# Gathered rows of a three-layer graph network: written-out layers, a ring of eight groups, and first groups that gather x itself

## The reference

```python
msg = relu((x[src] * edge_weight[:, None]) @ W_msg + b_msg)          # layer 0
agg = segment_sum(msg, dst, N)
x1  = layernorm(x + relu(agg @ W_out + b_out))
# layers 1 and 2, h = x1 and then the result of layer 1
msg = einsum('nd,rde->rne', h, W)[edge_type, src]
h   = relu(segment_sum(msg, dst, N) + h @ SW + b)
out = layernorm(x1 + h)                                               # after layer 2
```

## Time and profile before

| | |
|---|---|
| median of 3 runs | 7518.52 us (7510.16 to 7519.22) |
| span of the profiled execution, first to last instruction | 6622.7 us |
| own time of the profiled execution | not given apart from its span |
| runs' median less the profiled span | 895.8 us |
| POOL busy | 4948.3 us (75%) |
| PE busy | 3199.1 us (48%), mean granted clock 0.583 |
| DVE busy | 1746.3 us (26%) |
| ACT busy | 686.1 us (10%) |
| instructions executed | 52,372 |

### The profile page before, as it was taken

The page is one execution under the profiler, slowest core; times in us unless marked ns, Lnnn a source line. Parts: engine busy times, 40 slices in busy tenths (PEclk is TensorE's granted clock), DMA queues, the critical chain, the costliest instruction groups (busy, mean ns, idle before and its releaser), DMA issues. The chain is left out here.

```text
span 6622.7 us, 52372 instructions
## 1 busy us (share of the span) xinstructions
PE 3199.1 (48%) x12124; PEld 2491.7 (38%) x12124; DVE 1746.3 (26%) x4136; ACT 686.1 (10%) x2063; POOL 4948.3 (75%) x5004
## 2 busy tenths in 40 slices
PE   4455555555555444444445544443444444443443
PEld 4344444444444333333333333333333333333333
DVE  3344444444444311111111111111111111111112
ACT  1112222222222100000000000000000000000000
POOL 4777777777777677777777777767777777777776
PEclk7566666656666656666665666665555555555555
DMA  4122222222222222222222222221222222222222
GB/s 130 52 80 83 83 83 83 83 83 83 83 83 87 76 54 76 76 75 75 75 72 76 76 75 76 76 77 50 56 57 58 58 58 57 57 57 56 58 57 55
DMA packets 255517, 474.23 MB, mean 72 GB/s; under 512 B 90635, under 2 KB 143412, under 8 KB 255454
## 3 DMA queue, kind: packets, MB, share of 16 engines
q0 software_dynamic: 159744, 327.48, 19.1%
q1 hardware_dynamic: 92620, 144.65, 6.0%
q10 hardware_dynamic: 3090, 1.38, 0.1%
HBM read 351.16 MB, written 121.98 MB: 71 GB/s over the span
## 5 line engine op out<-in xcount | busy, mean ns | idle before, releaser
L576 POOL DMA_INDIRECT rows<-rel_table,index x3328 | 3306.4, 994 | 1070.0 <-issue 1009.7
L622 PE MATMUL bank<-onehot,rows 128*128 128x128 f32 x9984 | 2337.4, 408 | 3369.7 <-DMA rows<-rel_table,index 2340.9
L622 PEld LDWEIGHTS bank<-onehot,rows 128*128 128x128 f32 x9984 | 2024.6, 301 | 3668.2 <-DMA rows<-rel_table,index 1590.4
L576 POOL DMA_INDIRECT rows<-msg_table,index x1664 | 1629.8, 979 | 587.6 <-issue 583.3
L608 DVE TENSOR_TENSOR agg<-agg,bank 128x128 f32 x624 | 179.5, 288 | 3569.0 <-PE bank L622 3540.5
L596 DVE SCALAR_TENSOR_TENSOR rows<-rows,weight,bm 128x128 f32<-128x128 f32 x1664 | 474.6, 347 | 1146.8 <-DMA rows<-msg_table,index 1146.8
L584 DVE TENSOR_TENSOR onehot<-columns,place 128x1024 f32<-128x1024 f32 x624 | 765.8, 1227 | 19.6 <-issue 9.7
L819 PE MATMUL bank<-wr,feat 128*128 128x512 f32 x784 | 641.8, 969 | 3.5 <-ACT feat L767 2.4
L568 ACT ACTIVATE rows<-rows 128x512 f32<-128x512 f32 x416 | 261.8, 629 | 1657.9 <-DVE rows L596 1657.9
L819 PEld LDWEIGHTS bank<-wr,feat 128*128 128x128 f32 x784 | 236.9, 332 | 198.8 <-issue 194.6
L559 ACT ACTIVATE index<-rel_index 128x8 int32 (+1 forms) x416 | 85.4, 207 | 1546.4 <-DMA rows<-rel_table,index 1542.3
(11 more groups left out here) (65 smaller groups left out, 628.6 us busy)
## 6 DMA issues: line engine op xcount, KB each, us to landing
rel_table<-tab SPq DMA_DIRECT2D x196, 512.0 KB, 2.7
rows<-rel_table,index POOLq DMA_INDIRECT x3328, 2.5
rows<-msg_table,index POOLq DMA_INDIRECT x1664, 2.5
x_dram<-normed SPq DMA_DIRECT2D x98, 64.0 KB, 2.9
xin<-x_dram SPq DMA_DIRECT2D x98, 64.0 KB, 2.0
xin<-in_x_dram SPq DMA_DIRECT2D x97, 64.0 KB, 2.4
out_dram<-normed SPq DMA_DIRECT2D x97, 64.0 KB, 2.0
tab<-in_x_dram SPq DMA_DIRECT2D x24, 256.0 KB, 2.8
```

Of the source, the lines that this page charges most:

```text
L576: nc.gpsimd.indirect_dma_start(rows[:, st.u, t, :], None, table, bass.IndirectOffsetOnAxis(ap=index[:, st.u, t:t + 1], axis=0)).then_inc(s ...
L622: ins = nc.tensor.matmul(ps_edge[k][:, 0:P], rows[:, st.u, t, :], onehot[:, k, t, :], start=t == 0, stop=t == TPG - 1)
```

## The change

1. `RING` = 8: `rows` holds 8 groups. The second chunk of raw edges and the sheets' transposes now live in memory that is free at that time (`spare`, `raws[0][0]`).
2. All three layers are written out (`fused_loop` has no hardware loop), and so is `message_table`. POOL's gathers take their row numbers straight from `msg_index` or `rel_index` (`static_gather`). The executed path no longer uses `index`. The program has 26,781 instructions where it had 8447.
3. The first 8 groups (`EARLY`) gather rows of x, as soon as their numbers are laid out, ahead of the window check (`early_gathers`). On arrival PE transposes them and multiplies them by W_msg (`pe_convert`, `act_convert`), and DVE scales the product out of PSUM.
4. `columns` and `bm` are copied to PSUM (`ps_columns`, `ps_bm`, bank 5). `onehot` and the scaling of all groups but the first 8 read them there. `ps_a` is left with one bank, so a block's product waits for the `y` of the block before.
5. The layout copies src first, and transposes each part as soon as it is there; the window check comes after `message_table`. ACT zeroes `agg` in 25 pieces within `message_table`.

```diff
+RING = 2 * UNROLL
...
-        rows = sb("rows", [P, UNROLL, TPG, D])
+        rows = sb("rows", [P, RING, TPG, D])
...
-        ps_a = [bank[4], bank[5]]
+        ps_a = bank[4]
         ps_t = [bank[6], bank[7]]
+        ps_sheet = [bank[4], bank[5]]
+        ps_columns = bank[5][:, 0:P]
+        ps_bm = bank[5][:, P:P + D]
...
+                nc.vector.tensor_copy(f_src, e_src).then_inc(sems.flt, 1)
...
-                nc.vector.tensor_copy(f_src, e_src)
...
-        IDX_LEAD = 2
+        IDX_LEAD = 3
+        EARLY = RING
...
+        def static_gather(layer, g):
...
+            u = g % RING
+            table, table_index = ((rel_tables[layer - 1], rel_index) if layer else
+                                  (x if g < EARLY else msg_table, msg_index))
+            n = layer * GROUPS + g
+            need(nc.gpsimd, edge_main.prod, n - RING + 1)
+            pass_waits(nc.gpsimd, s_pool_turn)
+            for t in range(TPG):
+                nc.gpsimd.indirect_dma_start(
+                    rows[:, u, t, :], None, table,
+                    bass.IndirectOffsetOnAxis(ap=table_index[:, g, t:t + 1], axis=0)
+                ).then_inc(s_early[u] if n < EARLY else edge_main.rows[u][t // HALF], 16)
+
+        def early_gathers():
...
+            nc.gpsimd.wait_ge(lay.te, 2)
+            for g in range(EARLY):
+                if g == RING // 2:
+                    nc.gpsimd.wait_ge(lay.te, BATCHES * IN_ORDER)
+                    nc.gpsimd.wait_ge(lay.flag, 1)
+                static_gather(0, g)
+
+        def pe_convert(g):
...
+            for h in range(2):
+                i = 2 * g + h
+                if h == 0:
+                    nc.tensor.wait_ge(s_early[g], 16 * TPG)
+                need(nc.tensor, s_feat, i - 1)
+                for j in range(HALF):
+                    ins = nc.tensor.transpose(ps_t[h][:, j * P:(j + 1) * P],
+                                              rows[:, g, h * HALF + j, :], ident[:, :])
+                ins.then_inc(s_turned, 1)
+            for h in range(2):
+                i = 2 * g + h
+                nc.tensor.wait_ge(s_feat, i + 1)
+                need(nc.tensor, edge_main.scaled, i - 1)
+                for j in range(HALF):
+                    ins = nc.tensor.matmul(ps_tab[h][:, j * D:(j + 1) * D],
+                                           sheet_feat[:, h, j * P:(j + 1) * P], wm[:, :],
+                                           start=True, stop=True)
+                ins.then_inc(s_product, 1)
...
-                in0=columns[:, :].unsqueeze(1).to_broadcast([P, TPG, P]),
+                in0=ps_columns.unsqueeze(1).to_broadcast([P, TPG, P]),
...
-                            out=rows[:, st.u, t, :], in0=rows[:, st.u, t, :],
-                            scalar=w[:, 0, t:t + 1], in1=bm[:, :], op0=ALU.mult, op1=ALU.add)
+                            out=rows[:, st.u, t, :],
+                            in0=product if convert else rows[:, st.u, t, :],
+                            scalar=w[:, 0, t:t + 1],
+                            in1=bm[:, :] if convert else ps_bm, op0=ALU.mult, op1=ALU.add)
...
+                    piece = agg[:, st.b * ZERO:min((st.b + 1) * ZERO, NP + P)]
+                    eng.activation(piece, ones[:, 0:1].to_broadcast([P, piece.shape[1]]), ACT.Copy,
+                                   scale=0.0).then_inc(s_zero, 1)
...
-                need(nc.tensor, sems.xuse, st.n - 1)
+                need(nc.tensor, sems.xuse, st.n)
...
+            steps = GROUPS // PAIR if eng is nc.gpsimd else BLOCKS + LAG + LAST_STAGE[layer]
+            for s in range(steps):
+                at = At(s - s % UNROLL, s % UNROLL)
+                fused_edges(eng, layer, s)
+                if eng is nc.scalar and at.block(LAG, BLOCKS) is not None:
+
+                    eng.wait_ge(edge_main.added, min(s * PAIR + 1, GROUPS) + layer * GROUPS)
                 node_step(eng, layer, at, LAG)
...
-            eng.memset(agg[:, :], 0.0).then_inc(s_zero, 1)
+            early_gathers()
```

More of the change, by code:

```diff
@@ L36, with __init__ @@
 class Block:
-    def __init__(self, b, first, u):
+    def __init__(self, b, first, u, ring=UNROLL, early=0):
         self.b = b
         self.n = b + first
-        self.u = u % UNROLL
+        self.u = u % ring
+        self.early = early
 class At:
@@ L551, in gathered, with act_index @@
         def gathered(st):
-            return (st.n - st.u + UNROLL) * (16 * HALF // UNROLL)
-        def act_index(layer, sems, st, lead):
+            return (st.n - st.u + RING * (1 - st.early)) * (16 * HALF // RING)
+        def act_index(layer, sems, step, lead, first):
             table_index = msg_index if layer == 0 else rel_index
[L557 to L560, removed]
+            for q in range(PAIR):
+                k = step.u * PAIR + q
+                last = Block(step.b * PAIR + (q - RING), first, k, RING)
+                if isinstance(last.n, int) and last.n < 0:
+                    continue
+                for h in range(2):
+                    nc.scalar.wait_ge(sems.rows[k][h], gathered(last))
+            nc.scalar.activation(
+                index[:, step.u, :],
+                table_index[:, at_index(step.b * PAIR + lead, PAIR), :].rearrange(
+                    "p g t -> p (g t)"), ACT.Copy).then_inc(sems.index, 1)
         def act_relu(layer, sems, st):
@@ L581, in dve_group, with act_convert @@
+        def act_convert(g):
+            for h in range(2):
+                i = 2 * g + h
+                nc.scalar.wait_ge(s_turned, i + 1)
+                need(nc.scalar, s_product, i - 1)
+                nc.scalar.activation(sheet_feat[:, h, :], ps_t[h][:, :], ACT.Copy
+                                     ).then_inc(s_feat, 1)
         def dve_group(layer, sems, st, lead):
@@ L645, in edge_step @@
                 elif st is not None:
-                    if eng is nc.gpsimd:
-                        pool_gather(layer, sems, st, lead)
+                    if eng is nc.scalar:
+                        act_relu(layer, sems, st)
+                    elif eng is nc.gpsimd:
+                        pool_gather(layer, sems, st, at.block(0, steps, first // PAIR))
                     elif eng is nc.tensor:
@@ L732, in emit @@
                     ins.then_inc(s.prod, 1)
[L734 to L736 removed]
+            for n in range(SHEETS + (eng is nc.tensor)):
+                emit(At(n - n % UNROLL, n % UNROLL))
         PRODUCTS = (3, 0)
```

197 lines of the change are left out of this document (121 added, 76 removed).

## The result

| | before | changed |
|---|---|---|
| median of 3 runs | 7518.52 us (7510.16 to 7519.22) | 7324.3 us (7323.71 to 7329.33) |
| ratio | | 0.9747 [0.9729, 0.9764] |
| profiled execution: own time, span | not given, 6622.7 us | 7329.33 us, 7327.3 us |

The account below looks back on a forecast made before the run. The prediction took a chain of 4992 gathers on POOL to bound the kernel. Its terms, -70.5 - 197 + 3 = -264.5, taken from 7518.5, gave 7254.0 us, with a range of 7185 to 7400.

Parts of the forecast that it names:

- three signs of being wrong: Gathers' mean staying at 980 to 990, ninth group starting after 120, or runs' median and span moving by different amounts.
- start, to the ninth group: From the span's start to POOL's ninth gather group: starts at 103.5 instead of 174.02, -70.5 us, bounds -79 to -59.
- three strings of gathers: POOL's 1664 gathers in each layer: of 217 us in lengthened gathers, nine tenths go, -197 us.
- joints and tail: Waits for `rel_table` stores between layers, and the end after the last gathers: +2 in layer 0's end, +1 in tail.
- If they are added whatever the program does: The 895.8 us of the runs' median above the profiled span, taken as fixed: 7518.5 - 264.5 = 7254.0 us.
- part 2: One-hot with one input in PSUM stops lengthening POOL's gathers: -197 us, between 0 and -217.
- Part 1: First gather moves from 93.61 to about 11, beside the table; ninth group waits for group 0's product, 103.5: -70.5 us.
- The second rival: Early groups gain nothing: table and gathers fight for DMA engines until both end near 170; -194, 7324.5 us; chance 0.05.
- The stretch stays: Something else in the one-hot's time lengthens the gathers, so PSUM sources give nothing: -67.5, 7451.0 us; chance 0.10.
- Part 3: Single `ps_a` bank delays products at layer 0's end and in the tail: +2 and +1, 0 to 6 together.
- Part 4: Ring of 8 gives nothing by itself; leaving out registers and branches gains 0, more code costs 0.
- The third rival: Time outside the span, 895.8 us, grows with the program's 3.17 times more instructions to 2840: total 9198; chance 0.07.

Follow-up runs that it names:

- kernel 1: The kernel before, unchanged, profiled once more on a chip with late signals: 7515.06 us, span 7513.3 us.
- kernel 7: Changed kernel, POOL's gathers after the first 8 groups waiting for PE's product four groups before, not eight; chip without late signals: 6345.22 us, ratio 0.9624.
- 3: Changed kernel with one-hot and scaling reading columns and bias from SBUF again, first chip, late signals: 7343.62 us, ratio 0.9773 to before.
- 9: Changed kernel with one-hot and scaling reading columns and bias from SBUF again, third chip, late signals: 7385.79 us, ratio 0.9762 to before.
- experiment 6: Changed kernel, POOL also waiting for its gathers to land after every fourth group, second chip, no late signals: 6665.71 us.
- experiment 11: Changed kernel, POOL also waiting for its gathers to land after every fourth group, third chip, late signals: 7355.34 us, ratio 0.9723 to before.
- 2: Kernel before with `columns` and `bm` in PSUM and one bank for `ps_a`, first chip, late signals: 7565.65 us, ratio 1.0067.
- 10: Kernel before with `columns` and `bm` in PSUM and one bank for `ps_a`, third chip, late signals: 7594.85 us, ratio 1.0041.

## Why the prediction came out as it did

The changed kernel's time is in the range, on the side of the forecast, and 70 us above the number. In good part that is luck. Two of the three signs of being wrong that the prediction names came up in the profile after: the ninth group starts after 120, and the span moved by +704.6 us where the median moved by -194. The sum itself can now be laid beside two pairs of profiles, one of each kind of chip (gathers' starts from the earlier trace rows and the rows above, the ninth group before at 176.53; of kernel 1, that of experiment 1, the places are 183.94, 2577.35, 2615.01, 5046.02, 5066.39 and 7496.05). The two profiles of the first pair may be of different chips, since it is not told on which one the profile before was taken:

| term | predicted | no late signals: before to kernel 7 | late signals: kernel 1 to changed |
|---|---|---|---|
| start, to the ninth group | -70.5 | -58.9 | -29.6 |
| three strings of gathers | -197 | -222.6 | -211.3 |
| joints and tail | +3 | +5.1 | +54.9 |
| span | -264.5 | -276.4 | -186.0 |

**The step that failed** is "If they are added whatever the program does". The 895.8 us were taken as something outside the span that no part of the change could touch, and the sum was made on a profile in which POOL bounds the kernel. They were inside, 843 of them as idle time before gathers (experiment 1). On such a chip the length of POOL's work is not the bound, and each term has another price: part 2, put at 197 us, is worth 19 to 21 (experiments 3 and 9).

**Part 1.** Right in mechanism. On the prompt chip the first gather came at 10.68 (predicted 11) and the ninth group at 117.64 (bounds 95 to 115), but the ring of four of experiment 7 makes some 20 us of that. With the ring of eight experiment 6 has 99.67, stops included. The table began at 29.35 there, 8.7 us earlier than before (predicted 3, at most 6), and took 6.5 longer beside the gathers (predicted 6), so its last copy ends at 87.6 and not at 93. The way to the first product was summed wrongly: the steps listed, with their hand-overs, give 7.6 and not 9.5, and the multiplications in them are priced at half, since the 8 records of a row were taken for a whole group, which has 16. From PE's first transpose at 88.54 to the end of that product at 96.89 it took 8.35. On the chips with late signals the start is off: the table makes two sheets in 58 us beside the gathers, and its last copy comes at 145.5 instead of 93. The second rival (table and gathers fight for the DMA engines until both are late) has the measured time to 0.2 us, by chance, and the wrong cause; shares are 0.26 with the standstill and 0.81 without.

**Part 2.** Right in its mechanism, at every place looked at: 943 to 946 ns in the three layers with one input in PSUM, 979 to 1053 with both in SBUF. "The stretch stays" is out. Its price of 197 (nine tenths of 217 would be 195) can hold only where POOL sets the pace. There the strings lost 222.6: all of the stretch, 214.8 by the right ninth group, and 8 more from a pitch of 1.248. No run undid part 2 on that chip, so its price there is read from two profiles and not from an edit. With late signals it is worth 19 to 21 us (experiments 3 and 9). The 211.3 us that the strings lost there look like this term and are not it: with part 2 undone the time is still 0.9773 of before. The Trainium skill, "SBUF — State Buffer", section "Who interferes with whom", says that a VectorE instruction with two SBUF inputs shuts out a GpSimd instruction that reads SBUF, and that one with a single SBUF input, outside the two-port modes, does not; the traces agree with both halves now.

**Part 3.** The +3 is met without late signals in its sum (+5.1) but not in its parts: the first joint grew by 6.3 us, from 36.7 to 42.9 (38 predicted), and the tail became 1.1 shorter. With late signals the joints are 63.07 and 31.80 us against 37.66 and 20.37, and the tail 35.3 against 17.3: PE stands five or six groups behind POOL when a layer's gathers end, in kernel 1 one or two, and those groups are still to be done. So these +54.9 us and the shorter strings are in part one thing: with a ring of eight POOL runs further ahead and then waits longer. Counted at the end of each layer's last product, the changed kernel is 104 us ahead of kernel 1 after layer 0 and gains 40 and 42 in the other two.

**Part 4.** "A deeper ring gives nothing by itself" follows from a profile in which POOL hardly waits. With late signals the rest of the change (ring of eight, written-out code without `index` copies, early groups) carries nearly all of the gain, since only 19 to 21 us go with part 2. For the ring speaks that PE waits 1259.6 us for the rows of layers 1 and 2 in experiment 1 and 62.2 in the changed kernel. The missing `index` copies are a weaker candidate: in experiment 1 POOL waits 339.4 + 244.9 us for them, but in the changed kernel its idle time before gathers is no smaller, 2578.5 us against 2500.4. Ring and code were not tried apart on such a chip.

**The third rival**, a cost that grows with the program, is out: own time less span is 2.0 us after and 1.8 in experiment 1, and on the chip without late signals the time fell by 250.4 us with the long program.

**What stays open.** Why signals and matmuls of PE are late on two of the three chips. That POOL's gathers have a part in it is suggested by the start, and no more than that: late until POOL stops at 94.3, prompt from 104 on, with the same table code. In the layers POOL's stops and the signals' arrivals come together (3844.91 and 3848.21), but experiment 11 brings no faster pace with its stops, so the arrivals may as well be what ends the stops. That the DVE and PE round sets the pace there is argued from one trace, and five runs (2, 3, 9, 10 and 11) do not speak against it; the test would be a third slot of `onehot` and a third bank for the products, and was not made.

## What to carry to other kernels

Compare the profiled span with the runs' median first. If they differ by a tenth, the profile may show another state of affairs than the runs, and another engine may be the bound in them, so get a profile whose own time matches before pricing anything. An edit that is made for one question can move another place as well: the ring of four of experiment 7 moved the ninth group by some 20 us. And where signals come 20 to 30 us late, look first at loops of two engines with two buffers between them; here a gain of 5% on the engine that looks busiest brought 0.3% there.

## What the runs showed of the hardware

- The same kernel takes 7516 us on one chip, 7564 on another and 6596 to 6600 on a third. The difference is not TensorE's mean clock: the granted mean of the kernel before is 0.594 to 0.597 in its runs near 7516 and 0.582 to 0.586 in those at 6596.
- On the slower two, an add of layer 1 that follows the end of PE's product by 0.14 us in experiment 7 follows it by 14 on average and by up to 48.3 (changed kernel).
- A gather that is issued while DVE compares two SBUF tiles grows by up to 1.06 us; with one of the two in PSUM no gather behind the first eight groups takes over 1.01 us (changed kernel).
- Beside the standstill of the table, PE had a granted clock of 0.55, near the lower of its two levels (1.2 GHz), with 27 matmuls in 58 us, and 1.00 with 302 in the same window where signals are prompt. PE was busy for 6.1 of the 58 us in the first case and for 38.2 in the second.
